# Order of two DMA issues on the sync engine: the store of a turned block ahead of the load into the raw buffer

## The reference, cut to what matters

```
h = norm(x);  e = h + weighed(h)               # per row factor, 64x64 weights, users and items apart
x = x + layernorm(adj @ (adj.T @ e))*gamma + beta + h
h = norm(x);  x = x + adj @ h
h = norm(x);  T1 = adj @ h; T2 = 2*adj@T1 - h; T3 = 2*adj@T2 - T1
              x = x + h@w[0] + T1@w[1] + T2@w[2] + T3@w[3] + bias
h = norm(x);  x = x + relu(dis * ((adj + I) @ (dis * (h@W + b))))     # dis = (row sums of adj + 1) ** -0.5
```

## Time and profile before

| | |
|---|---|
| time, median of 3 runs | 1615.52 us (1612.44 to 1619.65) |
| the profiled execution's own time | 1620.43 us |
| its span, first to last instruction | 1618.6 us |
| mean granted TensorE clock | 0.986 |
| TensorE matmul busy | 1560.8 us (96%) |
| VectorE busy | 445.7 us (28%) |
| ScalarE busy | 274.6 us (17%) |
| GpSimd busy | 95.0 us (6%) |
| moved by DMA | 531.43 MB, mean 328 GB/s |

### The profile page before, as it was taken

How to read it: one execution, slowest core, us unless ns; L and a number is a source line. 1 busy time by engine, 2 the same in 40 slices (tenths; PEclk the granted TensorE clock), 3 DMA queues, 4 the chain that set the end, 5 groups by cost and what they waited for, 6 DMA issues and landing times.

```text
span 1618.6 us, 19966 instructions
## 1 busy us (share of the span) xinstructions
PE 1560.8 (96%) x8361; PEld 682.9 (42%) x8361; DVE 445.7 (28%) x583; ACT 274.6 (17%) x546; POOL 95.0 (6%) x103
## 2 busy tenths in 40 slices
PE   7899999999999988999999899999999999999698
PEld 4555555555555554333333333333333343333232
DVE  5485444444444335111111110001000031111211
ACT  2233343333433443000000000000000010000000
POOL 3200000000000028100000000000000000000000
PEclk9999999999999999999999999999999999999899
DMA  9699999999999999999788768887668737837997
GB/s 328 235 373 375 378 372 368 375 373 370 372 358 332 322 408 394 367 408 384 315 344 338 314 252 286 287 301 295 260 268 339 321 128 297 309 142 302 419 404 320
DMA packets 102858, 531.43 MB, mean 328 GB/s; under 512 B 19164, under 2 KB 19204, under 8 KB 55044
## 3 DMA queue, kind: packets, MB, share of 16 engines
q1 hardware_dynamic: 96068, 528.83, 84.9%
q10 hardware_dynamic: 6720, 1.58, 0.4%
HBM read 424.20 MB, written 106.17 MB: 328 GB/s over the span
## 4 chain that ended last, share of the span: by engine, by line
PE 82%; DMA 11%; ACT 2%; DVE 2%; issue 1%; POOL 1%; SPq 0%; ACTq 0%; DVEq 0%
PE turned L427 33%; PE acc L427 27%; DMA adj_t<-staged 9%; PE t_acc L439 8%; PE turned L453 8%; PE t_acc L574 2%; ACT staged L631 2%; DMA out_dram<-sq 1%; PE t_acc L594 1%; PE acc L476 1%; PE t_rows L584 1%; PE t_acc L576 1%; DMA raw<-in_adj_dram 1%; POOL rstd L922 0%; PE t_rows L490 0%
## 5 line engine op out<-in xcount | busy, mean ns | idle before, releaser
L631 ACT ACTIVATE staged<-turned 128x512 f32<-128x512 f32 x400 | 204.3, 614 | 303.5 <-PE turned L453 199.9
L754 DVE TENSOR_REDUCE deg_part<-raw 128x3072 f32 (+2 forms) x70 | 222.7, 3192 | 0.0
L453 PE MATMUL turned<-ident,raw 128*128 128x128 f32 x1600 | 206.8, 281 | 8.4 <-ACT staged L631 7.7
L453 PEld LDWEIGHTS turned<-ident,raw 128*128 128x128 f32 x1600 | 171.7, 141 | 62.3 <-issue 35.8
L439 PE MATMUL t_acc<-raw,E 128*64 128x384 f32 (+1 forms) x1120 | 188.2, 479 | 3.2 <-DMA raw<-in_adj_dram 3.2
L427 PE MATMUL acc<-staged,t_cur 128*64 128x512 f32 x800 | 189.3, 607 | 1.2 <-ACT t_cur L665 1.2
L427 PE MATMUL turned<-over_last,F 128*64 128x512 f32 x776 | 183.4, 600 | 0.0
L427 PE MATMUL turned<-over_last,E 128*64 128x512 f32 x752 | 177.0, 595 | 0.0
L922 POOL TENSOR_TENSOR rstd<-rstd,minus_half 128x4 f32<-128x4 f32 x50 | 51.7, 1035 | 1368.7 <-DVE rstd L743 1368.6
L439 PEld LDWEIGHTS t_acc<-raw,E 128*64 128x64 f32 x1120 | 80.0, 139 | 111.0 <-issue 86.7
L711 ACT ACTIVATE part<-turned 128x512 f32<-128x512 f32 x40 | 23.9, 597 | 549.9 <-PE turned L427 531.8
(11 more groups left out here) (120 smaller groups left out, 933.1 us busy)
## 6 DMA issues: line engine op xcount, KB each, us to landing
over_last<-adj_t SPq DMA_DIRECT2D x201, 1024.0 KB, 9.6
raw<-in_adj_dram SPq DMA_DIRECT2D x60, 1536.0 KB, 10.4
adj_t<-staged SPq DMA_DIRECT2D x60, 1536.0 KB, 13.2
staged<-adj_t SPq DMA_DIRECT2D x60, 1024.0 KB, 9.9
over_wide<-adj_t SPq DMA_DIRECT2D x42, 1024.0 KB, 10.1
raw<-in_adj_dram SPq DMA_DIRECT2D x10, 1024.0 KB, 9.3
adj_t<-staged SPq DMA_DIRECT2D x10, 1024.0 KB, 7.8
out_dram<-sq ACTq DMA_DIRECT2D x10, 128.0 KB, 15.0
```

The lines of the kernel that those rows point to most:

```text
L453: last = nc.tensor.transpose(bank[:, a * P:(a + 1) * P], raw_of(g, m)[:, a, c * P:(c + 1) * P], ident[:, :])
L631: nc.scalar.activation(staged_of(m)[:, c * B:(c + 1) * B], turned[(m * chunks(g) + c) % TURN_BANKS][:, :], ACT.Copy).then_inc(chunk_copied, 1)
L754: nc.vector.tensor_reduce(out, raw_of(g, m), AX.X, ALU.add).then_inc(deg_summed, 1)
```

## The change

In `group` of the sync engine's program the two calls change places. For each tile the store of (g, m) is now issued first, and the load of (g+1, m) behind it. Nothing else is edited; the waits inside the two functions are the same.

```diff
             def group(g):
                 for m in range(NB):
+                    store(g, m)
                     load_next(g, m)
-                    store(g, m)
```

## The result

| | before | after |
|---|---|---|
| time, median | 1616.68 us (1612.44 to 1619.86, 6 runs) | 1623.78 us (1621.89 to 1626.58, 6 runs) |
| the profiled execution's own time | 1620.43 us | 1622.34 us |
| its span | 1618.6 us | 1620.5 us |

The changed kernel takes 1.004 of the time, with a 95% interval of 1.0023 to 1.0056: 7.1 us more by the medians. So the profiles show where time moves, and single terms read from them are good to some microseconds.

A forecast was written before the change was run, and what follows sets the result against it. The prediction took the DMA engines as the bound between 147 and 487 us, 8.50 us per load-store pair. Groups two to five +5, first group +1.3, others 0: +6.3 on the 1615.5 us median, about 1622 us, range 1609 to 1637.

The forecast's parts named there:

- The store was late and its waits go; the load is late next: Loop steps: ScalarE's 103.5 us of store waits go, costing TensorE at most 6.1 us; TensorE then waits for loads.
- The load's landing: Loop step, store first: load lands at T + 11.56 (T: TensorE has turned a tile), due at T + 10.95.
- The ordinary step, 8.53 us: 36 steps of groups two to five without `turn_t`: 8.53 us instead of 8.50, +1.1 in all.
- A pair of one load and one store costs the DMA engines 8.50 us: Groups two to five before: 40 steps in 340.1 us at DMA share 1.00, taken as the engines' pace.
- TensorE's own pace of 8.22 us: Step of turn 2.91, multiply 2.73, products 2.58 us; 40 steps 334 us if nothing is waited for.
- Groups two to five: 40 steps: +1.1 from ordinary steps, +4.0 from four steps with `turn_t`, together +5 us.
- First group: Eight steps formerly at TensorE's 8.22 us become 8.38: +0.16 each, +1.3 us.
- Seventh group and later: Seventh group and later stages: same order of issues, moved as a whole, 0.
- Start: Store of tile 0 can be issued 16 us earlier, but nobody waits for it: 0.
- nothing changes: Rival: DMA engines full either way, order moves only who waits; +0, -2 to +3 us; chance 0.17.
- Faster: Rival: the pair gets cheaper, 3.8 + 3.9 = 7.7 us, load lands T + 10.8; -10 us, 1605.5; chance 0.12.
- Slower: Rival: load's delay paid in full with swings, decided where loads land later than about T + 12; +19, 1634 us; chance 0.26.

The follow-up runs named there:

- x3: Kernel before (load first) with TensorE forming each product of the next group one step later: 1619.89 us, 1.0006 of the kernel before.
- x4: Kernel before with store first only in the second to fifth column groups, load first elsewhere: 1623.44 us, 1.0022 of the kernel before.
- the best kernel: Changed kernel (store first) with products one step later and loops written out: 1599.12 us, 0.9872 of the kernel before.
- x6: Kernel before with the loops over groups two to five written out on TensorE, ScalarE and VectorE: 1614.98 us, 0.9973 of the kernel before.
- x2: Changed kernel (store first) with each product of the next group formed one step later: 1602.58 us, 0.9894 of the kernel before.
- x9: Kernel before with row block m of the turned matrix kept at place (m + 5) mod 10 in DRAM: 1619.05 us, 0.9999 of it.
- x1: Kernel before, load still first, but the load also waits for the last copy: 1641.12 us, 1.0137 of the kernel before.
- x11: The text ties this label to no one change; measured beside the kernel before at a median of 1619.49 us; its own time is not given by label.
- x5: Kernel before with store first only in the sixth column group: 1616.21 us, 0.998 of the kernel before.

## Why the prediction was right

The forecast was +6.3 us and the measured difference +7.1. Direction and mechanism hold: the store's lateness was mostly hidden, the load's is not. That the numbers lie so close is in part luck, for some terms were off in opposite directions, and the difference itself is known only to a few microseconds.

- **The store was late and its waits go; the load is late next.** Right, in the list of waits (103.5 us gone, 18.8 to 50.6) and by the two experiments that give the load slack, one in the schedule and one in bytes.
- **The load's landing.** Said T + 11.56, measured T + 11.1. The term that was off is the pair at 8.50 us: the load's own service is 3.9 us in this order and not 4.7. The fixed part of 2.2 us fits: 6.3 less 2.2 is 4.1 for the store.
- **The ordinary step, 8.53 us.** The mean measured is 8.53 too, by two errors that cancel. The landing was put 0.4 us too late. Products and turn behind it take 5.79 us in the timeline above and not 5.49: 2.80 for products that had to wait, 2.99 for the turn.
- **"A pair of one load and one store costs the DMA engines 8.50 us."** True of the order load, store as far as the runs show: with TensorE's own step shortened, groups two to five still took 340.2 us. Wrong as a price that the pair carries into the other order. There the same 40 pairs were moved at 8.33 us each with a share of 0.97, and at 7.6 where transfers had piled up. Even in the old order it is no constant: the first group ran at 8.22 with a share of 1.00, and in x3, load first too, loads issued at 424.41, 432.70 and 441.07 landed 9.1, 8.5 and 7.8 us later, that is 7.7 us apart.
- **TensorE's own pace of 8.22 us.** Right for the first group and wrong for groups two to five. There its turn takes 2.99 to 3.06 us, so its own 40 steps are 337.5 us and not 334; of the 340.1 only 2.6 were waits for transfers. Written out, the 2.91 us are back. What differs in the loop are the waits on register values; that they delay ScalarE's first copy is a guess that no run measured by itself.
- **Groups two to five.** Said +5, the two profiles show +7.0, and the order turned in these groups alone gave +4 (interval of the ratio: +1 to +6), and the table has +2 to +5 for x4. The split into +1.1 and +4.0 was wrong: the 8.50 was a mean that had the steps with `turn_t` in it, and it was used for the ordinary ones. The steps with `turn_t` take 9.35 us in both kernels, so nothing was lost in them but 2.5 us in one, and the ordinary ones went from 8.41 to 8.53.
- **First group.** Said +1.3, the two profiles show +3.2; other kernels with load first there take 65.7 to 67.8 us against 69.0. **Sixth group.** Said 0 between -4 and +4; 70.7 us lies inside what kernels with load first there take (68.5 to 72.9), so no difference is shown.
- **Seventh group and later.** Said 0, "moved as a whole". Wrong: 3.9 us less in the two profiles, and the experiment on the sixth group, -3 in all, has its gain here. What moved is ScalarE's wait for a store, which had stopped TensorE for 3.61 us. The prediction took the stop of 2.04 us for the largest one and didn't look behind 560 us.
- **Start.** Said 0; the profiles show -2.2, though not by the early store: TensorE stops for the first reloaded tile as before (2.98 and 3.08 us). In one it went on at full clock and in the other not, see below. I take it for spread, as the written-out kernel, unchanged there, has -2.6. But that nobody waits for the early store holds only as long as TensorE stops for the load; with later products it was worth 7 us.

Of the rivals, *nothing changes* is excluded by the interval, at its lower end of +3.7 by little. *Faster*, by a cheaper pair, had a true half: the load does get cheaper, to the 3.9 us named there, but that brings it to T + 11.1 and not to T + 10.8, and 0.15 us past the due time is a wait. With slack the same order gains 17 us. How much earlier the landing would have to be to turn the sign without slack was not tried; 1.9 us ahead of the due time ends the waits. *Slower* needed landings past T + 12, that is over 10.7 us after the issue, which some six of the 60 loads have.

## What to carry to other kernels

When two transfers share one queue, write down for each the landing time and the time at which it is due, and put first the one that is late, if the other can afford the first one's whole service. If it can't, first make slack for it (here: use the loaded tile one step later), since the same order was +7 us without the slack and -17 us with it. A DMA share of 1.00 with a constant pace gives the price of the transfers in the order that was traced; in another order it can be another (370 and 404 GB/s here, both at full share). And follow a change of order to where the queue is next waited for: here 3.9 us lay behind the last transfer that was moved.

## What the runs showed of the hardware

**The order on one queue changes what a load costs.** Loads are 4.7 us behind the store ahead of them when load goes first and 3.9 when store goes first, at the same sizes; with all engines busy the second order moved 404 GB/s for 49 us in the best kernel; the first 370 over groups two to five, and 388 at most over a first group (x6). Shifting the addresses changed nothing, splitting the stores around the load cost 10 us, two queues cost 43. What happens inside is open; no run here tests it.

**Issuing a load sometimes takes long.** With the load right behind the store, SP's issue of it took 0.38 us as a rule and 1.45 to 2.22 in four of the 60; before, none was over 0.37. With later products (x2) none was. It doesn't make a load late by itself: two of the four landed after 9.9 and 10.4 us. The changed kernel's costliest stop, 2.27 us of TensorE's, is for a load that was issued in 0.38 us at 227.78 and landed after 12.1.

**The clock after a stop.** After 3.08 us of idle TensorE, the window 70 to 80 us of the kernel before shows a granted clock of 0.83 (part of it at the lower level, 1.2 instead of 2.4 GHz), and the 16 products took 4.22 us. After 2.98 us of idle time in the changed kernel it shows 1.00, and they took 2.80. Other kernels have the same stop: 2.20 us in x6 with 1.00; 3.10 in x9 and 3.14 in x1 and x11 with 0.83; 3.06 in x4 and 3.32 in x5 with 0.66 and 5.39 us for the products. So this stop alone makes executions differ by up to 2.6 us, and the two profiles compared here fell on different sides. The windows, before and then after:

```profile
70.00:80.00 10.00, 6.92 (x38) 3.30 (x34) 7.16 (x4) 1.13 (x3) 9.92 (x2) 0.83 1.04 422
```

```profile
70.00:80.00 10.00, 7.02 (x48) 4.09 (x48) 6.44 (x3) 3.05 (x6) 9.86 (x3) 1.00 0.89 363
```
